# A state-space mixer with a ternary feed-forward: the order of the feed-forward steps, and the end of the last two tiles

## The reference

```python
def activation_quant(x):      # per row
    s = 127 / clip(max(abs(x), axis=-1), 1e-5)
    return clip(round(x * s), -128, 127) / s
def weight_quant(w):          # per matrix
    s = 1.0 / clip(mean(abs(w)), 1e-5)
    return clip(round(w * s), -1, 1) / s
...
x = x + mixer(ctx_1024, layernorm(x))        # (4, 512, 512)
n = layernorm(x)
h = silu(bit_linear(n, w_gate)) * bit_linear(n, w_up)   # (.., 2048)
h = rms_norm(h, ln_weight)
out = x + bit_linear(h, w_down)
```

## Time and profile before

| | us |
|---|---|
| median of 3 runs (lowest, highest) | 626.03 (624.44, 628.39) |
| profiled execution, whole | 625.08 |
| its span | 623.3 |
| busy in the span: PE, DVE, ACT, POOL | 547.6, 542.2, 512.6, 467.1 |

### The profile page before, as it was taken

One profiled execution on the slowest core, in us unless ns is written; L12 is line 12 of the kernel. 1 busy time (PEld: TensorE's weight loads), 2 busy tenths in 40 slices (PEclk: granted clock), 3 DMA queues, 4 the chain that ended last, 5 costly groups with the idle time before them and its releaser, 6 DMA issues.

```text
span 623.3 us, 10096 instructions
## 1 busy us (share of the span) xinstructions
PE 547.6 (88%) x3598; PEld 403.1 (65%) x3598; DVE 542.2 (87%) x807; ACT 512.6 (82%) x749; POOL 467.1 (75%) x181
## 2 busy tenths in 40 slices
PE   5978976799999999999998899987889889979974
PEld 2423665799998999899997899852334334334321
DVE  3999676999999999999999999967887988988760
ACT  3897898999999999999997999969667756765750
POOL 3583882999999999999999999944454655565551
PEclk9986778899999999999999899999989999999988
DMA  9984352111212641236311762444332432352332
GB/s 295 411 318 144 119 219 67 51 53 52 69 52 85 154 135 52 68 92 181 99 56 54 177 192 64 126 108 76 78 60 59 94 85 60 77 101 59 80 82 67
DMA packets 67345, 69.68 MB, mean 112 GB/s; under 512 B 46304, under 2 KB 46304, under 8 KB 65120
## 3 DMA queue, kind: packets, MB, share of 16 engines
q1 hardware_dynamic: 64992, 64.68, 35.9%
q0 software_dynamic: 2304, 4.36, 4.2%
HBM read 50.02 MB, written 8.52 MB: 94 GB/s over the span
## 4 chain that ended last, share of the span: by engine, by line
POOL 23%; ACT 22%; issue 19%; PE 15%; DVE 15%; DMA 4%; SPq 0%; POOLq 0%; DVEq 0%
POOL arena L455 10%; POOL arena L489 10%; ACT arena L644 10%; ACT arena L640 7%; DVE arena L746 5%; DVE arena L835 4%; PE ps L1121 4%; PE ps L1105 3%; POOL arena L499 3%; PE ps L1021 2%; DVE arena L923 2%; PE ps L1108 2%; DMA arena<-c_rows 2%; ACT arena L637 1%; PE ps L1155 1%
## 5 line engine op out<-in xcount | busy, mean ns | idle before, releaser
L455 POOL TENSOR_TENSOR arena<-arena 128x2048 f32<-128x2048 f32 x63 | 286.7, 4598 | 16.5 <-DVE arena L835 15.1
L835 DVE TENSOR_TENSOR_SCAN arena<-arena,ps 128x512 f32<-128x512 f32 x256 | 286.8, 1198 | 6.3 <-PE ps L1108 4.4
L644 ACT ACTIVATE arena<-arena,a_neg 128x512 f32<-128x512 f32 x256 | 164.7, 709 | 7.9 <-DVE arena L835 7.8
L1121 PE MATMUL ps<-ident,arena 128*128 128x128 f32 x1024 | 155.6, 275 | 5.4 <-DVE arena L845 3.3
L1121 PEld LDWEIGHTS ps<-ident,arena 128*128 128x128 f32 x1024 | 120.8, 142 | 9.2 <-POOL arena L455 4.7
L1155 PE MATMUL ps<-arena 128*128 128x512 bf16 x512 | 114.0, 379 | 3.9 <-DVE arena L923 3.4
L1108 PE MATMUL ps<-ident,arena 128*128 128x128 f32 x640 | 98.1, 278 | 10.5 <-ACT arena L640 8.1
L1105 PE MATMUL ps<-arena 128*128 128x128 f32 x768 | 103.0, 278 | 3.3 <-ACT arena L640 2.8
L640 ACT ACTIVATE arena<-arena,bT 128x512 f32<-128x512 f32 x160 | 102.0, 709 | 3.9 <-DVE a_neg L825 2.5
L1105 PEld LDWEIGHTS ps<-arena 128*128 128x128 f32 x768 | 94.3, 194 | 4.9 <-ACT arena L640 3.0
L489 POOL TENSOR_TENSOR arena<-arena 128x1024 f32<-128x1024 f32 x32 | 77.6, 2424 | 25.4 <-DVE arena L923 25.4
(11 more groups left out here) (96 smaller groups left out, 580.0 us busy)
## 6 DMA issues: line engine op xcount, KB each, us to landing
...
arena<-ctx_t SPq DMA_DIRECT2D x4, 512.0 KB, 12.3
```

The lines of the kernel that those rows point to most:

```text
L455: nc.gpsimd.tensor_tensor(hs[:, k % RING, :, :], hs[:, k % RING, :, :], c_bc[:, s:s + 1, :].to_broadcast([P, KE, L]), ALU.mult).then_inc(S ...
L644: nc.scalar.activation(dA[:, s, i, :], delta_u[:, b, 0, i, :], ACT.Exp, scale=a_neg[:, i, n:n + 1]).then_inc(S["dA_ready"], 1)
L835: nc.vector.tensor_tensor_scan(out=hs[:, k % RING, i, :], data0=dA[:, k % 2, i, :], data1=ps[:, 4 + i, :], initial=0.0, op0=ALU.mult, op1= ...
L1121: last = mm(ps[:, c, i * P:(i + 1) * P], hs[:, k % RING, i, c * P:(c + 1) * P], ident[:], start=(n == 0 and i == 0), stop=(n == DS - 1), i ...
```

## The change

- GpSimd weighs both halves of tile t, and then adds x to tile t-2. The last tile is weighed in four quarters; the additions of tiles 13 and 14 stand behind its power.
- VectorE: scale_rows is split. scale_hidden (the scale aq of tile t-1) comes first and alone, then scale_row (the x side) with a wait behind each step. cut_x moves ahead of the fourth product. In the last tile the maxima are taken of a half and two quarters, the sum of squares comes in two parts, and one instruction scales the down result and adds x.
- ScalarE: round_x moves ahead of the fourth silu. scale_down and cut_down of the last two blocks move forward. In the last tile the square and L707 are done in halves.
- Tiles 14 and 15 are not turned by DMA: TensorE transposes q2 against a bf16 identity into PSUM as bf16 (tile 14 into two banks at once, tile 15 in two halves), and ScalarE, or VectorE for the last half, copies them to q2T. The down projections of these two run in halves behind the copies.

The declarations of semaphores and buffers, the one-line copy of the identity and the body of the removed scale_rows are cut; of unchanged lines only the neighbours stand.

```diff
@@ -154,13 +155,19 @@
-        half_max = sb("half_max", [P, 2])
+        half_max = sb("half_max", [P, 3])
+        ssq_end, var_end = sb("ssq_end", [P, 1]), sb("var_end", [P, 1])
+        ps_q = ps[:, 6:8, :].rearrange("p a n -> p (a n)").bitcast(BF16).rearrange("p (k n) -> p k n", k=KI)
+        def ps_end(half):
+            return ps[:, half, :].bitcast(BF16).rearrange("p (k n) -> p k n", k=KI // 2)
@@ -189,7 +196,8 @@
         ACT_SUMMED, DVE_SUMMED = (4, 5, 5), (0, 3, 7)
         DVE_CUT, ACT_CUT = ((0, 1), (0, 2), (1, 0)), ((0, 0), (0, 3), (1, 1), (1, 2), (1, 3))
-        FFN_STEPS = range(0, TILES + 2)
+        FFN_STEPS = range(TILES)
+        END = TILES - 1
         def hold(eng, *waits):
@@ -370,14 +378,17 @@
             load_down(2)
             def store_out(t):
-                sp.wait_ge(S["fin_done"], t + 1)
+                if t == END:
+                    sp.wait_ge(S["fin_end"], 1)
+                else:
+                    sp.wait_ge(S["fin_done"], t + 1)
                 sp.dma_start(out_v[:, t, :], o_s[:, t % 2, :]).then_inc(out_stored[t % 2], 16)
...
                     store_out(t - 3)
-                if tile(t - 1):
+                if tile(t - 1) and t - 1 < END - 1:
                     turn_q(t - 1)
@@ -488,18 +499,32 @@
                 w = slice(half * 1024, half * 1024 + 1024)
                 nc.gpsimd.tensor_tensor(p2[:, s, w], h2[:, s, w], lnw[:, w], ALU.mult).then_inc(S["p2_ready"], 1)
+            def weigh_end(j):
+                hold(pool, "h_ready", END * 4 + j + 1, "q_ready", END - 1)
+                w = slice(j * 512, j * 512 + 512)
+                nc.gpsimd.tensor_tensor(p2[:, END % 2, w], h2[:, END % 2, w], lnw[:, w],
+                                        ALU.mult).then_inc(S["p2_ready"], 1)
+            def add_rows(t):
+                pool.wait_ge(S["down_scaled"], t + 1)
+                nc.gpsimd.tensor_tensor(o_s[:, t % 2, :], o_s[:, t % 2, :], x_all[:, t, :],
+                                        ALU.add).then_inc(S["fin_done"], 1)
             pool.wait_ge(S["lnw_loaded"], 16)
...
                     power(EARLY + t + 1, 0 if tile(t + 3) else 1, 2 if tile(t - 1) else 1)
-                if tile(t):
+                if t < END:
                     weigh(t, t % 2, 0)
-                if tile(t - 2):
-                    pool.wait_ge(S["down_scaled"], t - 1)
-                    nc.gpsimd.tensor_tensor(o_s[:, t % 2, :], o_s[:, t % 2, :], x_all[:, t - 2, :],
-                                            ALU.add).then_inc(S["fin_done"], 1)
-                if tile(t):
                     weigh(t, t % 2, 1)
+                    if tile(t - 2):
+                        add_rows(t - 2)
+            for j in range(NJ):
+                weigh_end(j)
+            power(EARLY + END + 2, 1, 2)
+            add_rows(END - 2)
+            add_rows(END - 1)
@@ -676,6 +701,13 @@
...
                 cut_down(n)
+            scale_down(2)
+            def scale_rows(t):
+                hold(act, "down_psum", t + 1, out_stored[t % 2], t // 2 * 16)
+                nc.scalar.activation(o_s[:, t % 2, :], ps[:, DOWN_BANK[t % 2], :], ACT.Copy,
+                                     scale=dsc[:, t:t + 1]).then_inc(S["down_scaled"], 1)
             def silu(t, j):
@@ -686,6 +718,8 @@
...
                     silu(t, 0)
+                if t == 0:
+                    cut_down(2)
@@ -693,30 +727,42 @@
...
                 if t == 0:
-                    scale_down(2)
-                    cut_down(2)
+                    scale_down(3)
                 if tile(t):
                     silu(t, 2)
-                if t < 2:
-                    if t == 0:
-                        scale_down(3)
-                    else:
-                        cut_down(3)
+                if t == 1:
+                    cut_down(3)
+                if t == END:
+                    hold(act, "h_ready", END * 4 + 2)
+                    nc.scalar.activation(sq_out[:, 0:1024], h2[:, END % 2, 0:1024], ACT.Square,
+                                         accum_out=ssq[:, END:END + 1]).then_inc(S["ssq_ready"], 1)
                 if tile(t - 1):
...
                                          scale=aq[:, t - 1:t]).then_inc(S["tq_ready"], 1)
+                if tile(t + 2) and t + 2 >= EARLY:
+                    round_x(t + 2)
                 if tile(t):
                     silu(t, 3)
-                if tile(t + 2) and t + 2 >= EARLY:
-                    round_x(t + 2)
                 if tile(t + 3):
...
                 if tile(t - 2):
-                    hold(act, "down_psum", t - 1, out_stored[s], (t - 2) // 2 * 16)
-                    nc.scalar.activation(o_s[:, s, :], ps[:, DOWN_BANK[s], :], ACT.Copy,
-                                         scale=dsc[:, t - 2:t - 1]).then_inc(S["down_scaled"], 1)
+                    scale_rows(t - 2)
+            hold(act, "h_ready", END * 4 + 4)
+            nc.scalar.activation(sq_out[:, 1024:], h2[:, END % 2, 1024:], ACT.Square,
+                                 accum_out=ssq_end[:]).then_inc(S["ssq_end_ready"], 1)
+            act.wait_ge(S["qT_psum"], 1)
+            for half in range(2):
+                k = slice(half * 8, half * 8 + 8)
+                nc.scalar.activation(q2T[:, (END - 1) % 2, k, :], ps_q[:, k, :], ACT.Copy).then_inc(S["qT_copied"], 1)
+            act.wait_ge(S["aq_ready"], END + 1)
+            for half in range(2):
+                w = slice(half * 1024, half * 1024 + 1024)
+                nc.scalar.activation(p2[:, END % 2, w], p2[:, END % 2, w], ACT.Identity, bias=magic[:],
+                                     scale=aq[:, END:END + 1]).then_inc(S["tq_ready"], 1)
+            act.wait_ge(S["qT_psum"], 2)
+            nc.scalar.activation(q2T[:, END % 2, 0:8, :], ps_end(0), ACT.Copy).then_inc(S["qT_copied"], 1)
+            scale_rows(END - 1)
         @block.vector
@@ -821,6 +867,7 @@
...
             keep_duT(3, 1)
+            nc.vector.tensor_copy(identb[:], ident[:]).then_inc(S["identb_ready"], 1)
             dve.wait_ge(S["act_consts"], 1)
@@ -868,42 +915,36 @@
-            def scale_rows(x, h):
...
+            def scale_hidden(h):
+                one = slice(h, h + 1)
+                dve.wait_ge(S["rstd_ready"], EARLY + h + 2)
                 own.wait()
+                own.done(nc.vector.tensor_scalar(crm[:, one], rstd2[:, 1:2], scales[:, h, 1:2], None, ALU.mult))
+                if h == END:
+                    own.done(nc.vector.tensor_scalar(amax[:, one], half_max[:, 0:1], half_max[:, 1:2],
+                                                     half_max[:, 2:3], ALU.max, ALU.max))
+                else:
                     own.done(nc.vector.tensor_scalar(amax[:, one], half_max[:, 0:1], half_max[:, 1:2], None, ALU.max))
                 own.wait()
+                step(nc.vector.tensor_scalar(mx[:, one], amax[:, one], crm[:, one], Q_EPS, ALU.mult, ALU.max))
+                step(nc.vector.reciprocal(aq[:, one], mx[:, one]))
+                nc.vector.tensor_scalar(aq[:, one], aq[:, one], crm[:, one], 127.0, ALU.mult,
+                                        ALU.mult).then_inc(S["aq_ready"], 1)
+                own.done(nc.vector.tensor_scalar(dsc[:, one], mx[:, one], 1.0 / 127.0, wmean[:, 2:3], ALU.mult,
+                                                 ALU.mult))
+            def scale_row(x):
                 own.wait()
+                dve.wait_ge(S["xn_ready"], x + 1)
+                step(nc.vector.tensor_reduce(out=am[:], in_=xn(x), axis=AX.X, op=ALU.max, apply_absolute_value=True))
+                step(nc.vector.tensor_scalar(am[:], am[:], Q_EPS, None, ALU.max))
+                own.done(nc.vector.reciprocal(s1[:], am[:]))
+                for w in range(2):
+                    own.done(nc.vector.tensor_scalar(scales[:, x, w:w + 1], wmean[:, w:w + 1], am[:], 1.0 / 127.0,
+                                                     ALU.mult, ALU.mult))
                 own.wait()
+                step(nc.vector.tensor_scalar(s1[:], s1[:], 127.0, None, ALU.mult))
+                dve.sem_inc(S["s1_ready"], 1)
             def cut_x(t):
                 dve.wait_ge(S["x_rounded"], t + 1)
@@ -917,6 +958,12 @@
                     out=half_max[:, half:half + 1], in_=p2[:, t % 2, half * 1024:half * 1024 + 1024], axis=AX.X,
                     op=ALU.max, apply_absolute_value=True))
+            def biggest_end(part_of, first, last):
+                dve.wait_ge(S["p2_ready"], END * 2 + last)
+                own.done(nc.vector.tensor_reduce(
+                    out=half_max[:, part_of:part_of + 1], in_=p2[:, END % 2, first * 512:last * 512], axis=AX.X,
+                    op=ALU.max, apply_absolute_value=True))
             def gated_up(t, j):
@@ -956,24 +1002,52 @@
...
                 x_row = t + 2 if tile(t + 2) and t + 2 >= EARLY else None
-                if tile(t - 1) or x_row is not None:
-                    scale_rows(x_row, t - 1 if tile(t - 1) else None)
+                if tile(t - 1):
```

(69 more changed lines are left out.)

34 lines of the change are left out of this document (3 added, 31 removed).

## The result

The changed kernel takes 597.61 us (median of 4 runs, 595.33 to 599.93) against 626.25 (4 runs): a ratio of 0.9542, 95% interval 0.9494 to 0.959. The prediction was 600.2 us, in a range of 596 to 610. Its profiled execution took 597.98 us, with a span of 596.2, which is 27.1 us shorter. Run a second time beside some of the experiments (e12), it took 596.68 us, so a difference of less than 1 us between groups of runs says nothing.

A forecast was written before the change was run, and what follows sets the result against it. No engine was full; a ring of waits set the 12.02 us tile. An 18.4 us earlier last product plus 7.5 from the tail, less 0.1, gave 25.8 off 626.03: 600.2 us, range 596 to 610.

The forecast's parts named there:

- the walk: VectorE's steps through one tile, from second product to the next tile's: 10.72 us, taken as 10.8 a tile.
- the tightest cover: GpSimd's power behind the addition, done at 11.0 when the scale asks at 11.3: 0.25 us of slack.
- The sum: Whole kernel: 18.4 us from an earlier last product plus 7.5 from the tail, less 0.1: 25.8 us gained.
- the middle: L707 of tile 0 to that of tile 12: 12 tiles of 10.8, 129.6 us, where it was 145.5.
- the last tiles: After L707 of tile 12, TensorE's queue sets the pace; last product at 580.85, where it was 599.29.
- The reading of the ring: Whole tile: a ring of waits sets its 12.02 us; step to attack is GpSimd's addition ahead of the weighing.
- TensorE's floor: TensorE in one tile: down projection 3.47 us and gate and up 7.07, about 10.7 with the joints.
- Rival A: Middle tiles: full VectorE and TensorE rings hinder each other, 11.4 us a tile, about 607 us; chance 0.2.
- Rivals B and C: B: GpSimd's power late, tile near 12, 614 us, chance 0.1. C: turn_q landing grows, about 630 or more, 0.03.
- Start: First tile: weight blocks scaled and cut earlier on ScalarE, L707 at about 426.9 instead of 430.01, 3.1 us.
- End: Last product to end of span: 15.6 us, 16.5 with a clock allowance, against 24.0; gain 7.5 us.
- half clock: Last down projections: one slow group costs 1.7 us, half of it added; both at 1.2 GHz makes the tail 19.

The follow-up runs named there:

- e12: The changed kernel itself, run a second time beside some experiments: 596.68 us, ratio 0.9517 to the kernel before.
- e1: Changed kernel, but GpSimd adds x to the finished tile between the two weighings again: 603.45 us, ratio 0.963 to the kernel before.
- e4: Kernel before with one edit, GpSimd weighs both halves and then adds: 627.37 us against 626.33, ratio 1.002.
- e8: Changed kernel, but each VectorE maximum of a half reads 512 of its 1024 columns: 594.95 us, ratio 0.9488 to the kernel before.
- e9: Changed kernel, but the down projection of tiles 0 to 13 has 8 of its 16 matmuls: 598.19 us, ratio 0.9539 to the kernel before.
- e7: Changed kernel, but scale_down and cut_down of the third and fourth weight block back where they were: 599.59 us, ratio 0.958 to the kernel before.
- e11: Changed kernel with VectorE's x-side maximum, small steps and bn_stats moved to fill waits, complete work: 600.04 us, ratio 0.9559 to the kernel before.
- e3: Changed kernel, but cut_x stands behind the maximum of the first half again: 610.52 us, ratio 0.9749 to the kernel before.

## Why the prediction was right, and where it was not

**The end of the walk, 10.72 us, was near, but VectorE is not what sets the tile.** The tile is 10.61. VectorE's own sequence is 10.52: cut_x holds it for 0.33 (452.37 to 452.70), not 0.52, and the other terms came out within 0.1. The walk had the sum of squares ready at 8.8, 0.2 us before VectorE asks at 9.0; as VectorE asked earlier, this cover went, and the ring through ScalarE's queue sets the tile. The prediction named GpSimd's power, with 0.25 us, as the tightest cover, though by its own figures that of the squares was smaller. In the trace the power ends at 457.7, 0.6 before the scale starts at 458.3.

**The sum** was 25.8 us; the medians differ by 28.6. Counted from the end of the scan, the profiles differ by 28.0, of which 1.2 us more than forecast are the end, 0.5 the middle and 0.2 each the start and the last tiles.

**The reading of the ring was right for the chain and wrong for the lever.** "The step to attack is the addition ahead of the weighing": that ring was there, and putting it back costs 5.8 us (e1). Yet alone the edit gives nothing (e4). The prediction costed cut_x at 0.52 because it had moved, and said what it would cost if GpSimd ran over it; it did not say that the new weighing order is what puts GpSimd over the old place of cut_x. The three orders undone one by one cost 5.8, 10.3 and 12.9 us, 29.0 in sum, where all together, with the start, bring 20.3. They are not parts of a sum: what one order is worth depends on the others standing. For the addition that is shown both ways, nothing alone and 5.8 us in company; for the other two only the second half is.

**Late tiles.** TensorE's floor was given as 10.7 for a tile, from durations with their joints; it is 10.36 (e8, and the last down projections of the changed kernel, 554.70, 565.06, 575.42). The prediction counted twelve tiles of 10.8, 129.6 us, and 129.1 were measured, but with another shape: ten tiles of 10.5 to 10.6 and two of 11.5 and 11.6. That it came so close is in part luck: 0.2 too much for each of ten tiles made up for two long ones that the sum did not have. With one long tile, in e12, it was 128.1.

**Rival A happened, in two tiles of twelve.** A transpose that landed after 6.0 us instead of 4.3 made TensorE late, and these tiles about 0.95 us longer: 1.9 us in all. e9, with less for TensorE to do, has no such tile; but its only late landing (5.9 us, issued at 557.27) came behind the middle tiles, so it doesn't show whether a TensorE with time to spare would have borne one.

In the DMA windows of both long tiles (452 to 459 and 538 to 545 us) one packet of the instruction queue q8 stands beside the transposes. The queue's row in the first of them (packets, MB, share):

```profile
q8 instruction: 1, 0.02, 0.8%
```

Such packets come every 25 to 40 us all through the stage, and most of them meet no transpose in flight: in the changed kernel those near 482, 514 and 568 us fell between two, and no tile there is long. In the profiles of both kernels, e12, e1 and e7 to e11 there are fourteen that came some 2 us or more behind the issue of a turn_q and ahead of its landing, and these fourteen transposes are the ones that landed after 5.3 to 6.1 us; no other took over 4.9. In e12 the packet that could have made the second long tile came at 537.5 to 538.1, just as the transpose was issued (537.80), and that one landed after 4.3. So the coincidence is close in nine profiles, but no run moved or removed the packet: that it delays the transpose is not shown as a cause.

The prediction's price for this rival has a slip: 600.2 and 7.2, less 1.5, is about 606, not 607.

**Rivals B and C.** The addition and the power were never late. turn_q1 is issued 1.4 to 2.1 us behind turn_q (e.g. 452.48 and 454.29), not 0.6, and did not stretch a normal landing of turn_q: the median is 4.3 as before. Its own landing grew, from 2.5 us in the median and 3.5 at most to 3.0 and 4.6.

**Start.** 3.1 us were predicted, 3.3 measured. By e7 2.0 (medians) to 2.5 of them (profiles) are the weights' cuts; the rest is put down to the orders.

**End.** Predicted 16.5, measured 15.3. The 0.85 us set aside for half clock was not needed, and two prices were too high: 16 bf16 transposes took 1.05 us, not 1.6, and VectorE's copy of 1024 bf16 columns from PSUM 0.69, not 1.2. Copies on ScalarE (0.96 each) and the L741 halves (2.37 for both) came as estimated.

**The port and the clock.** Under the weighing cut_x took 1.68 us (e3) and 1.67 (e4) and ended 0.3 us behind it, against 0.42 in the clear. The Trainium skill (SBUF — State Buffer, on the port that VectorE and GpSimd share) says that a two-port VectorE instruction and a GpSimd one block each other for a whole instruction; the trace agrees.

The changed kernel kept the full clock across its gap of 2.9 us with transposes in it; e8 lost it across the same gap and e9 across 4.9. The Trainium skill (TensorE: Matmul & The Clock Gate, Part 4: PE-mode transpose) says that full rate doesn't engage for transposes, from which the prediction estimated an end of 19 us. It was 15.3, with a granted clock of 1.00 across the transposes. These runs don't show why the clock stayed, and the 15.3 us rest on it: with the half clock of e8 the end would have been about 1.7 us longer.
